# Graph network kernel, first loop: a DMA keeps the slot destinations, and ScalarE multiplies three more buckets of the third weight part

## The reference

```python
def hyp_agg(x, src, dst, w, c, n_nodes):
    xt = logmap0(x, c)
    msg = xt[src] * w[:, None]
    agg = jax.ops.segment_sum(msg, dst, num_segments=n_nodes)
    return proj(expmap0(agg, c), c)
...
h = jnp.maximum(_layernorm(x, axis=-1), 0.0)
x = x + _L0_gnn_ref(h, edge_index, edge_weight, ...)   # two layers with hyp_agg
h = jnp.maximum(_layernorm(x, axis=-1), 0.0)
x = x + _L1_gnn_ref(h, edge_index, ...)                # edge network: relu, segment mean
```

## Time and profile before

| what | value |
|---|---|
| median of the runs | 1180.15 us (3 runs, 1179.14 to 1183.04) |
| profiled execution | 1182.7 us |
| its span, first to last instruction | 1181.0 us |
| mean granted TensorE clock | 0.944 of full speed |
| first loop | about 72 to 477 us of the span |

### The profile page before, as it was taken

The page is one execution under the profiler, slowest core; times in us unless marked ns, Lnnn a source line. Parts: engine busy times, 40 slices in busy tenths (PEclk is TensorE's granted clock), DMA queues, the critical chain, the costliest instruction groups (busy, mean ns, idle before and its releaser), DMA issues.

```text
span 1181.0 us, 53889 instructions
## 1 busy us (share of the span) xinstructions
PE 1032.8 (87%) x21722; PEld 951.6 (81%) x21722; DVE 1050.3 (89%) x1400; ACT 720.7 (61%) x1981; POOL 687.1 (58%) x317
## 2 busy tenths in 40 slices
PE   3079999999999999628997599999999999999998
PEld 2058888888888888527997579999999999999997
DVE  8879999999999999685664879999999999999995
ACT  5348888888888889420002575555665565566663
POOL 7005788888888888100000037777777777777774
PEclk9569999999999999659998779999999999999999
DMA  2002322223232323669950255444444454444550
GB/s 82 0 34 96 127 112 109 120 102 122 99 126 95 127 95 127 269 245 331 420 211 31 87 169 164 156 159 162 162 155 161 150 159 157 160 162 162 162 162 29
DMA packets 44877, 169.98 MB, mean 144 GB/s; under 512 B 19440, under 2 KB 19766, under 8 KB 44827
## 3 DMA queue, kind: packets, MB, share of 16 engines
q1 hardware_dynamic: 44827, 169.28, 40.0%
HBM read 121.11 MB, written 48.14 MB: 143 GB/s over the span
## 4 chain that ended last, share of the span: by engine, by line
PE 61%; DVE 18%; ACT 12%; issue 6%; DMA 1%; DVEq 1%; POOL 1%; ACTq 0%; SPq 0%; POOLq 0%
PE PS L1573 18%; PE PS L1575 12%; ACT arena L666 8%; PE PS L1588 8%; PE PS L1446 8%; PE PS L1429 5%; PE PS L1593 3%; DVE arena L1076 3%; PE PS L1408 3%; DVE arena L1053 2%; DVE arena L1061 2%; DVE arena L1039 1%; DVE arena L1048 1%; PE PS L1477 1%; PE PS L1555 1%
## 5 line engine op out<-in xcount | busy, mean ns | idle before, releaser
L608 POOL TENSOR_TENSOR arena<-arena 128x512 bf16<-128x512 f32 x240 | 341.8, 1441 | 323.2 <-ACT arena L794 323.2
L582 POOL TENSOR_TENSOR aggTw<-aggTw,arena 128x72 f32 x48 | 318.2, 6630 | 132.2 <-ACT arena L677 132.2
L1573 PE MATMUL PS<-arena 125*128 125x128 bf16 x3600 | 343.4, 219 | 0.9
L794 ACT ACTIVATE arena<-arena 128x512 bf16<-128x512 f32 x240 | 150.8, 628 | 186.0 <-DVE arena L1295 186.0
L1573 PEld LDWEIGHTS PS<-arena 125*128 125x128 bf16 x3600 | 249.7, 97 | 7.4 <-issue 4.6
L666 ACT ACTIVATE arena<-arena 128x72 bf16<-128x72 bf16 x864 | 217.2, 341 | 4.3 <-DVE arena L1061 1.9
L1446 PE MATMUL PS<-arena,A 125*64 125x72 f32 x4800 | 179.0, 229 | 29.2 <-DVE A L957 25.7
L1446 PEld LDWEIGHTS PS<-arena,A 125*64 125x64 f32 x4800 | 164.4, 138 | 36.1 <-issue 28.0
L1295 DVE SCALAR_TENSOR_TENSOR arena<-PS,arena 128x512 f32<-128x512 f32 x240 | 159.4, 679 | 28.7 <-ACT arena L801 28.7
L801 ACT ACTIVATE arena<-PS 128x512 bf16<-128x512 f32 (+2 forms) x336 | 171.7, 546 | 1.2 <-PE PS L1575 1.2
L1575 PE MATMUL PS<-arena 108*128 108x128 bf16 x1200 | 166.7, 220 | 0.0
(11 more groups left out here) (197 smaller groups left out, 1397.4 us busy)
## 6 DMA issues: line engine op xcount, KB each, us to landing
adjacency<-arena SPq DMA_DIRECT2D x48, 900.0 KB, 3.7
arena<-adjacency SPq DMA_DIRECT2D x46, 900.0 KB, 8.0
Bw<-slot_rows SPq DMA_DIRECT2D x48, 800.0 KB, 4.2
Cw<-slot_rows SPq DMA_DIRECT2D x48, 700.0 KB, 4.5
arena<-q_table SPq DMA_DIRECT2D x144, 18.0 KB
q_table<-arena SPq DMA_DIRECT2D x6, 336.0 KB
slot_rows<-slot_row SPq DMA_DIRECT2D x49, 13.0 KB
x_sb<-in_x SPq DMA_DIRECT2D x1, 700.0 KB
```

The source lines that it names most:

```text
L582: nc.gpsimd.tensor_tensor(win, win, taken[k], ALU.add).then_inc(added, 1)
L608: nc.gpsimd.tensor_tensor(H3[k][:, at_b, 2, :], Hs[k][:, 4 * q:4 * q + 4, :], H3[k][:, at_b, 1, :], ALU.subtract).then_inc(s_low_set, 1)
L794: nc.scalar.activation(H3[k][:, at_b, 1, :], Hs[k][:, 4 * q:4 * q + 4, :], ACT.Copy).then_inc(s_mid_set, 1)
L1573: mm(ps, OTs[k][:, b, :], P3[:, b, part, :], start=(part == 0), stop=False)
```

## The change

`slot_dst` is no longer written by a copy on ACT. SP sends a DMA of 128 partitions x 50 bf16 numbers from field 1 of `slots` to `slot_dst`, behind the DMA of the transposed row, and `row_stored` counts both. Since that DMA reads `slots`, ACT's wait for `row_saved` moves from `take_rows` to `take_slots`, which overwrites that buffer two groups later. In `slot_weights` DVE makes part 3 for 4 buckets in place of 7, and in `third_weights` ACT makes it for 21 in place of 18. `third_set` thus counts four steps for each group in place of three, and PE waits for it in all four chunks.

```diff
+ON_VECTOR = 4
...
-                sp.wait_ge(row_stored, 16 * (g + 2))
+                sp.wait_ge(row_stored, 32 * (g + 2))
...
                 sp.dma_start(last.rearrange("g (b s) -> (g b) s", s=NS), slot_row[k][:, :])\
                     .then_inc(row_stored, 16)
+                sp.wait_ge(slots_set, nth(g))
+                sp.dma_start(slot_dst[:, bass.ds(g, 1), :, :].rearrange("p g b d -> p (g b d)"),
+                             slots[k][:, 1, 0:NB, :].rearrange("p b d -> p (b d)")).then_inc(row_stored, 16)
...
             def take_slots(g, k):
                 sc.wait_ge(slots_done, nth(g))
                 sc.wait_ge(onehots_set, nth(g - 2))
-                nc.scalar.activation(slot_dst[:, bass.ds(g, 1), :, :].rearrange("p g b d -> p (g b) d"),
-                                     slots_ps[:, 1, 0:NB].unsqueeze(2).broadcast_to([128, NB, 2]), ACT.Copy)
+                sc.wait_ge(row_saved, nth(g - 2))
...
-                for bs in CHUNKS[1:]:
+                for bs in [CHUNKS[0][ON_VECTOR:]] + CHUNKS[1:]:
                     for b in bs:
                         last = nc.scalar.activation(WD[k][:, 2, b, :], OD[:, b, :], ACT.Copy, scale=third[k][:, b:b + 1])
                     last.then_inc(third_set, 1)
...
             def take_rows(g, k):
                 sc.wait_ge(row_done, nth(g))
-                sc.wait_ge(row_saved, nth(g - 2))
...
             def slot_destinations(g, k):
-                ve.wait_ge(third_set, nth(3 * g - 1))
+                ve.wait_ge(third_set, nth(len(CHUNKS) * g - 1))
...
             def slot_weights(g, k):
-                for c, n in ((2, CB), (0, NB), (1, NB)):
+                for c, n in ((2, ON_VECTOR), (0, NB), (1, NB)):
...
             def blocks(g, k):
-                    if c:
-                        pe.wait_ge(third_set, nth(3 * g + c - 1))
+                    pe.wait_ge(third_set, nth(len(CHUNKS) * g + c))
```

More of the change, by code:

```diff
@@ L436, in _ @@
                 store_rows(0, 0)
-                sp.wait_ge(row_stored, 16)
+                sp.wait_ge(row_stored, 32)
                 sp.sem_inc(row_saved, 1)
```

## The result

The changed kernel takes 1209.75 us (median of 6 runs, 1206.64 to 1212.01), beside 1181.88 us for the kernel before (median of 6, its three runs more than in the table). The ratio is 1.0231, with a 95% interval from 1.0217 to 1.0246: slower by 27.9 us. The profiled execution took 1209.61 us, its span is 1207.9 us, 26.9 us longer than before.

The account below looks back on a forecast made before the run. DVE was taken as the bound at 8.40 us a group, with ACT's ring with PE at 8.255; 48 x 0.647 less 4.8 us of slack gave 26.3 us, so 1180.15 + 26.3 = 1206.5 us, range 1201 to 1212.

Parts of the forecast that it names:

- closed ring: First loop: ACT's multiplies, slots copy, PE's transpose and blocks, ACT's evictions wait in turn; 8.255 us against DVE's 8.40.
- The rival in which ACT's idle time takes the work: First loop: ACT's 0.81 us idle a group absorbs the added 0.647, DVE stays the bound; 1174.8 us, chance 0.04.
- the one in which the ring shrinks as it is loaded: First loop: PE's blocks or ACT's instructions get faster under load; about 1181 us, chance 0.03.
- The ring's own pace: First loop's start, where ACT is late: six groups between L666 starts at 84.11 and 133.64, 8.255 us each.
- Three multiplies, 0.737 us: ACT, each first-loop group: three more multiplies at 0.246 us of queue time each, together 0.737 us.
- The copy, 0.09 us: ACT, each first-loop group: removing the copy into `slot_dst` gives back 0.09 us, not its listed 0.20.
- DVE's 0.112 us: DVE's smaller multiply, each first-loop group: 216 elements less save 0.112 us, worth nothing since DVE waits for ACT.
- about 46.5: First loop, profile after: DVE busy about 46.5 us of 50, no longer 50, waiting for ACT's copy into `slots`.
- PE's added wait: PE, between transpose and first block in the first loop: bounded between 0 and 0.05 us, taken as 0.
- the sum of 26.3: Whole first loop: 48 groups x 0.647 = 31.1 us, less 4.8 us of ACT's slack, is 26.3 us.
- The DMA, 0 us: SP's queue, first loop: the new DMA hides in SP's 4.1 us idle a turn and costs 0.
- The clock: First loop: rival that more PE idle time lowers PE's clock; 1218 us if one turn in eight slows, chance 0.04.

Follow-up runs that it names:

- the ring opened: The whole change with PE's transpose of the next slots moved behind the block matmuls and ACT's copy of it behind the evictions: 1175.82 us, ratio 0.9958 to the kernel before.
- the split but ACT's copy: The changed kernel without its DMA: ACT multiplies 21 buckets and again copies the slot destinations; 1212.63 us, ratio 1.0268 to the kernel before.
- six buckets: The changed kernel with 6 buckets of part 3 on DVE in place of 4, so 19 multiplies on ACT: 1185.81 us, ratio 1.0036 to the kernel before.

## Why the prediction was right

- **The bound.** The prediction held that ACT and PE form a closed ring, only 0.145 us shorter than DVE's turn, so that ACT's idle time could not be used. The four kernels with 19 or 21 multiplies in the old order have turns of 8.43, 8.92, 8.89 and 9.01 us (L669 or its like in the second and in the last group, 46 turns apart); the ring gives 8.44, 8.93, 8.90 and 9.02 when 0.03 us is counted for the added wait where it is there. With the ring opened the same 21 multiplies fit into 8.29 us. That is the test that the argument rested on. The rival in which ACT's idle time takes the work falls, so does the one in which the ring shrinks as it is loaded, and so does any reading by which ACT simply had too much to do. The ring's own pace, read from six turns, is that of 46 turns in the kernel with DVE's smaller multiply alone (8.254 us).
- **Three multiplies, 0.737 us.** The 21 of the first group start at 73.83 and the copy behind them at 78.99, 5.16 us, for 4.42 before: 0.74.
- **The copy, 0.09 us.** The kernel with the split but ACT's copy has turns of 9.01, the changed one 8.92: 0.09. The page "ScalarE: Activation LUTs" of the Trainium skill (section What ACT_TABLE_LOAD costs) would have given 0.135 as an estimate; the measurement decides for 0.09.
- **DVE's 0.112 us.** Confirmed in size by the kernel that has it alone, and worth nothing in the changed one, where DVE waits for ACT. The forms with the new size, and the one beside it that surprised, in the changed kernel:

```profile
L1070 DVE TENSOR_TENSOR arena<-rampb,slots 128x3200 bf16<-128x3200 bf16 x45 | 87.6, 1946 | 0.0
...
L1078 DVE TENSOR_TENSOR arena<-arena,slots 128x288 bf16<-128x288 bf16 x45 | 13.3, 295 | 0.0
```

The 295 ns are as forecast. DVE is busy 47.5 us of 50 and not about 46.5, and waits 0.42 us and not 0.6, mostly because L1070 has grown from 1.81 us to 1.95, which was not foreseen. It lies in DVE's idle time.
- **PE's added wait, taken as 0, bounded at 0.05.** It is 0.03 by the profile, 1.4 us in 46 turns. It is the one term of the sum that is known to have been too small. The span is 26.9 us longer, 0.6 more than the sum of 26.3, so the other terms were 0.8 us too high together, which is less than the 5 us by which the runs of one kernel differ.
- **The DMA, 0 us.** Confirmed by the kernel that has it alone. The prediction let SP's idle time of 4.1 us hide it. But that idle time gave only 0.2 us (3.9 in the kernel with the DMA alone); most of the DMA went into the wait that SP has for the adjacency store, 2.7 us a turn before and 1.6 with the DMA.
- **The clock.** It stayed at 1.00 between 250 and 300 us, with PE idle 1.12 us a turn ahead of the transpose. This rival fell by the profile of the changed kernel; no run here tells how much idle time it would take.

The forecast of 1206.5 us was 3.2 us under the median, and the range of 1201 to 1212 holds it. Of these 3.2 us, 1.7 are in the median of before, which is 1181.88 over six runs and was 1180.15 over the three that the forecast started from; the rest is PE's wait and the spread of the runs.

## What to carry to other kernels

Idle time on an engine is no room until it is known where it stands. Here ACT idled 0.81 us a turn, but waiting for matmuls that had been waiting for ACT; whatever was put ahead of the copy lengthened ACT's own turn by all of it, and the loop's turn by all but 0.145 us. A stretch in which the engine is behind and catches up shows its own pace, and the difference to the bound's pace is the real slack, 0.145 us a turn here. To move work onto such an engine, take the instruction that closes the ring out of it first: moving one transpose behind the blocks turned 28 us of loss into 5 to 6 us of gain. And where two engines have turns of nearly the same length, busy time does not tell which one sets it: with six buckets DVE was busy throughout, and yet the turn was, as far as the trace tells, the ring's.

## What the runs showed of the hardware

POOL's add of a 128 x 72 window (L586, before L582) took 7.25 us at the median before and 1.15 in the changed kernel, and 0.31 at the loop's end, where DVE was idle. Before, it began among DVE's instructions on tables in SBUF (at 255.63) and ended at 262.87, 0.25 us after the start of L1048, whose input is in PSUM. In the changed kernel it starts 0.09 us after DVE has come out of its wait, ends in 1.20 us at 261.29, and the L1070 that starts at 261.02 is the one that takes 1.96 us and not 1.81. The page "GPSIMD Engine Reference" of the Trainium skill (section Specifications) says that POOL shares its SBUF interface with DVE, with contention against DVE instructions that have two inputs in SBUF. The long add agrees with this, as does its end at L1048. With DVE's smaller multiply alone the add began at places up to 1.3 us apart in DVE's turn (it takes 5.7 us at 112 us and 7.0 at 450) and still ended 0.26 to 0.29 us after the start of L1048 in all of the turns looked at (at 112, 252, 260 and 450 us). In the kernel with six buckets it is long and short in turn over most of the loop:

```profile
256.41 5.36 POOL L586 TENSOR_TENSOR aggTw<-aggTw,arena 128x72 f32 x1 [7.17 <-ACT arena L679]
264.89 1.23 POOL L586 TENSOR_TENSOR aggTw<-aggTw,arena 128x72 f32 x1 [3.11 <-ACT arena L679]
```

The first begins 0.07 us ahead of L1063, the second 0.06 us behind its start, and the L1070 after the second takes 1.96 us, the one after the first 1.81. So no wait of DVE that the profile shows is needed for the short form. Why such an add gets through among instructions that hold up the others stays open. POOL was not in the ring in any kernel here.

The issue of the new DMA, with 128 pieces of 100 bytes, held SP's queue 0.98 us (the row at 255.51 above), that of the adjacency store of 900 KB 0.35 us.
